# One exponential over three PSUM banks instead of two over two and one, in the attention of an encoder stage

## The reference, cut to what matters

```python
# per layer, x: [16, 256, 128], H = 16 heads, HD = 8
q, k, v = x @ Wq + bq, x @ Wk + bk, x @ Wv + bv     # split into heads
w = softmax(q @ k^T / sqrt(HD), masked)
x = ln(x + (w @ v) @ Wo + bo)
x = ln(x + gelu(x @ W1 + b1) @ W2 + b2)
```

## Time and profile before

| | |
|---|---|
| median of three runs | 5588.78 us (5578.2 to 5590.6) |
| profiled execution, its own time | 5589.84 us |
| its span | 5588.0 us |
| PE busy | 4103.1 us, 73% |
| DVE busy | 2823.0 us, 51% |
| ACT busy | 1910.5 us, 34% |
| POOL busy | 781.6 us, 14% |
| L951 (exponentials), 768 instructions | 580.2 us busy, 529.1 us idle before them |
| L543 (their scores), 3072 matmuls | 403.2 us busy, 80.0 us idle before them |
| L812 (row maxima), 1152 instructions | 747.1 us busy, 356.4 us idle before them |

### The profile page before, as it was taken

How to read it: one execution, slowest core, us unless ns; L and a number is a source line. 1 busy time by engine, 2 the same in 40 slices (tenths; PEclk the granted TensorE clock), 3 DMA queues, 4 the chain that set the end, 5 groups by cost and what they waited for, 6 DMA issues and landing times. The chain is left out here.

```text
span 5588.0 us, 74115 instructions
## 1 busy us (share of the span) xinstructions
PE 4103.1 (73%) x27895; PEld 2767.4 (50%) x27895; DVE 2823.0 (51%) x6809; ACT 1910.5 (34%) x2953; POOL 781.6 (14%) x1090
## 2 busy tenths in 40 slices
PE   5887888888878878879996447885333265887895
PEld 3565665656656656656664114553222233333663
DVE  4655646656556556522213778762455655112662
ACT  2454444544534544433333332212111112221441
POOL 1221222122222212200000000000000022002221
PEclk7998998999989989989997667985565566998995
DMA  4323314224134233000000000000000000002320
GB/s 120 90 52 95 86 49 100 65 72 100 41 94 101 53 85 82 16 35 0 0 0 12 0 0 1 1 1 0 4 0 0 0 3 21 0 0 53 89 70 19
DMA packets 157810, 224.88 MB, mean 40 GB/s; under 512 B 17838, under 2 KB 138030, under 8 KB 140078
## 3 DMA queue, kind: packets, MB, share of 16 engines
q10 hardware_dynamic: 19656, 107.37, 8.6%
q1 hardware_dynamic: 137870, 113.64, 7.4%
HBM read 157.37 MB, written 63.57 MB: 40 GB/s over the span
## 5 line engine op out<-in xcount | busy, mean ns | idle before, releaser
L812 DVE TENSOR_REDUCE enc_mx<-psum 128x2 f32<-128x512 f32 (+1 forms) x1152 | 747.1, 684 | 356.4 <-PE psum L524 353.2
L951 ACT ACTIVATE enc_e<-psum 128x1024 f32<-128x1024 f32 (+1 forms) x768 | 580.2, 808 | 529.1 <-PE psum L543 528.1
L524 PE MATMUL psum<-enc_ks,enc_qs 80*128 80x128 bf16 (+1 forms) x3072 | 475.0, 260 | 112.9 <-DVE enc_mx L812 98.3
L543 PE MATMUL psum<-enc_qs,enc_ks 83*128 83x256 bf16 (+1 forms) x3072 | 403.2, 259 | 80.0 <-DMA enc_qs<-max_pieces 54.3
L524 PEld LDWEIGHTS psum<-enc_ks,enc_qs 80*128 80x128 bf16 x3072 | 227.8, 102 | 244.6 <-DVE enc_mx L812 152.5
L543 PEld LDWEIGHTS psum<-enc_qs,enc_ks 83*128 83x128 bf16 x3072 | 269.4, 103 | 133.8 <-DMA enc_qs<-max_pieces 62.7
L554 PE MATMUL psum<-enc_e,enc_v 128*32 128x256 f32 (+1 forms) x6144 | 334.0, 335 | 0.0
L1608 PEld LDWEIGHTS psum<-par_s,moe_act_h 128*128 128x128 f32 x2304 | 268.6, 192 | 26.8 <-issue 26.8
L1595 PE MATMUL psum<-cur,par_s 128*128 128x512 f32 x576 | 274.0, 622 | 0.0
L68 POOL TENSOR_TENSOR rstd<-vareps,minus_half 128x4 f32<-128x4 f32 x40 | 40.3, 1007 | 1665.8 <-DVE vareps L50 1665.8
L1608 PE MATMUL psum<-par_s,moe_act_h 128*128 128x128 f32 x2304 | 271.5, 275 | 0.0
(11 more groups left out here) (432 smaller groups left out, 8126.4 us busy)
## 6 DMA issues: line engine op xcount, KB each, us to landing
enc_qs<-q_pieces ACTq DMA_DIRECT2D x234, 192.0 KB
enc_ks<-k_pieces ACTq DMA_DIRECT2D x234, 192.0 KB
k_pieces<-enc_pieces SPq DMA_DIRECT2D x240, 128.0 KB, 2.0
q_pieces<-enc_pieces SPq DMA_DIRECT2D x144, 128.0 KB, 2.0
enc_qs<-q_pieces SPq DMA_DIRECT2D x54, 192.0 KB
enc_ks<-k_pieces SPq DMA_DIRECT2D x54, 192.0 KB
rope_qs<-q_pieces ACTq DMA_DIRECT2D x39, 192.0 KB
rope_ks<-k_pieces ACTq DMA_DIRECT2D x39, 192.0 KB
```

The source lines that it names most:

```text
L524: last = T_.matmul(p1[f % 2][:, i * kw:(i + 1) * kw], qs[0:KEYED, slot, h, j * P:(j + 1) * P], ks[0:KEYED, slot, h, 0:kw], start=True, sto ...
L543: last = T_.matmul(p2[ch][:, g], ks[0:SCORED, slot, 4 * T + g, ch * P:(ch + 1) * P], qs[0:SCORED, slot, 4 * T + g, 0:n], start=True, stop= ...
L812: V.tensor_reduce(mx[:, u % 2, j * HEADS + h0:j * HEADS + h0 + n], p1[f % 2].rearrange("p (h k) -> p h k", h=n), AX_X, ALU.max)\
L951: A.activation(e_of(T, ch), p2[ch], ACT.Exp, scale=HD ** -0.5).then_inc(s_e, 1)
```

## The change

`expo` waits once, for both parts of the scores, and makes one activation over the 1536 columns of banks 2, 3 and 4, into the 1536 columns of the half of `enc_e`. It raises `s_e` by two when it is done. `HT * (S + P)` is 4 * 384 = 1536, and column 1024 is where bank 2 begins.

```diff
--- before.py
+++ after.py
@@ -946,9 +946,8 @@
             def expo(layer, u, T):
                 if 4 * u + T >= 2:
                     act.wait_ge(s_pv, at(layer, SEQS * HT, 4 * u + T - 1))
-                for ch in range(JT):
-                    act.wait_ge(s_p2, at(layer, 128, 8 * u + 2 * T + ch + 1))
-                    A.activation(e_of(T, ch), p2[ch], ACT.Exp, scale=HD ** -0.5).then_inc(s_e, 1)
+                act.wait_ge(s_p2, at(layer, 128, 8 * u + 2 * T + 2))
+                A.activation(e[:, T % 2], c.psum[:, 1024:1024 + HT * (S + P)], ACT.Exp, scale=HD ** -0.5).then_inc(s_e, 2)
 
             def move_sums(layer, u, half):
                 act.wait_ge(s_pv, at(layer, SEQS * HT, 4 * u + 2 * half + 2))
```

## The result

The change makes the kernel slower: 5619.53 us as the median of six runs (5610.01 to 5639.43), against 5588.23 (5572.43 to 5590.6, six runs) for the kernel before. The ratio is 1.0065, with a 95% interval of 1.0043 to 1.0086, so 24 to 48 us. The direction is the one forecast, and the size about twice: 15 us were forecast from median to median, and 31 came. The profiled execution took 5610.01 us, the fastest of the six, with a span of 5608.2 us, 20.2 more than before; so the profile shows less than the medians do.

A forecast was written before the change was run, and what follows sets the result against it. Waits, not ScalarE's busy sum, were taken to bound the encoder, even sequences waiting for the fetched maxima. 9.9 + 0.8 + 3.2 = 13.9 us on the profiled 5589.84 gave 5603.7; forecast 5603.5 as a median, range 5586 to 5620.

The forecast's parts named there:

- The instruction: One 1536-column exponential was put at 1453 ns, taken as 1.45 us; ScalarE frees 22 us over 384 blocks, at waiting work.
- The lateness of L940: Block 2, even sequences: the move of the next sequence's maxima comes 0.39 us later (0.38 median), delaying the next start.
- Block 0 costs nothing: Block 0: the one exponential is dispatched at the same 1255.65; 2.4 us of issuing six loads cover its end; no cost.
- From block 2 to the next start: Even sequences 0 to 12: 9.9 us from 26 places where the fetch follows its store by 1.4 us, 0.8 from four.
- the twelve held-up ones: Even sequences whose fetch follows its store by 1.8 to 3.4 us: counted as nothing, upper bound 4.6 us.
- Block 3's scores 0.2 late by their banks: 36 even sequences: block 3's scores wait for banks 2 and 3 and start 0.2 us late, beside the maxima wait.
- block 1's chain over L936 and L796: Block 1, even sequences: L936, L796 and reductions move by 0.38 us, block 3's scores by up to 0.38; covered.
- Sequence 14: No new maxima to make there; L940 and the next sequence come 0.54 us late, six times: 3.2 us.
- Sequence 15: Block 3's scores move 0.64 us, covered by 1.24 us of idleness: nothing, or 3.8 us if that cover is gone.
- odd sequences: Odd sequences 3 to 13: block 3's scores have 2.52 us where 1.6 are needed, maxima 1.2 to spare; no cost.
- a lower clock: Named beside a slower rival: a longer idle stretch can lower TensorE's granted clock, 0.93 in the encoder; no size given.
- every block pays: Rival: odd sequences have no slack either, 36 us, with 5 for sequences 14 and 15: 5631 us; chance 0.16.

The follow-up runs named there:

- split in block 2 alone: The change in blocks 0, 1 and 3, with two exponentials kept in block 2: 5595.6 us against 5587.4 for the kernel before, ratio 1.0015.
- the odd-sequence run: The kernel before with the one exponential in the odd sequences alone: 5591.7 us against 5593.8 for the kernel before, ratio 1.0001.

## Why the prediction was right in sign and short in size

**The instruction** (1453 ns, 22 us freed to no use) was right: 1451 ns, 21 us, and the wait alone without it costs as much.

**The lateness of L940** (0.38 to 0.39) was right in kind and came out as 0.42, since the exponential starts 0.12 us behind the scores instead of 0.09. That this lateness is what passes from block 2 to the next sequence is shown by four runs: merged in block 2 alone, split in block 2 alone, and the maxima moved to either side.

**Block 0 costs nothing: wrong, and the clearest failure.** I argued that the one exponential is dispatched at the same time as the second one before, and that 2.4 us of issuing cover its end. The end is covered; the start of the issuing is not. The load behind it went out 0.10 us later, and everything in block 0 hangs on that issuing, not beside it. By an estimate from the shortest sequences that is 36 x 0.10 = 3.6 us; summed over all 36 it can't be read, since single sequences differ by 1 us either way from profile to profile.

**From block 2 to the next start**, the sum had 9.9 for the 26 clean fetches, 0.8 for four, and nothing for the twelve held-up ones: 10.7 us. Against the one profile of before, the two of the change grew by 12.8 and 12.7, 0.9 and 1.1, and 1.7 and 2.5 us, 15 to 16 in all. But that profile has the lowest sum of the five that keep this part as it was; against their mean the growth is 11 us. The same holds for what the later store saves: the excess of store-to-fetch over 1.40 us, summed over the 42, is 14.9 to 20.2 us in those five (17.4 on average) and 12.4 and 12.2 with the change, so 2.6 us are absorbed by the first count and 5 by the second, where I had let 5.3 go. That the held-up fetches took in most of their lateness was right; whether the term was short at all is not shown.

**Block 3's scores 0.2 late by their banks**: they are 0.34 late, by block 1's chain over L936 and L796, which I had named as the other path. Neither reaches the end, as predicted.

**Sequence 14** 3.2 us: 3.3 and 4.0. **Sequence 15** and the **odd sequences** nothing: no cost of theirs is seen.

**The sum** with these sizes is 9 to 16 for block 2, 3.6 for block 0 and 3.3 to 4.0 for sequence 14: 16 to 24 us, where I had 13.9. The timings gave 31 and 29 us, 25 of them at an equal clock. So the step that failed is, as far as the runs show, the term for block 0 that I put at nothing; 1 to 9 us of the 25 have no term, and why the granted clock was lower in the runs of the change stays open, with the 5 us or so that go with it. I had named a lower clock beside a rival and given it no term of its own. The forecast's range reached to 5620, and the median lies under that by half a microsecond, which is luck. Of the rivals, "every block pays" gave the nearer number for a reason that the odd-sequence run refutes.

## What to carry to other kernels

Before two instructions are merged, look at what waited for the first one's inputs alone, and at what stands behind the second on the same engine: a merge moves the start to the later input, and what stands behind it in the queue moves too. Here the freed time was worth nothing, since ScalarE waited for its inputs in 307 of 384 blocks, and what it freed it spent waiting. And when an engine's queue also issues transfers, look at what stands behind the issuing and what the issuing waits for: here the same profile that gave 0.4 us a sequence to think about showed 3.87 us called issue in front of one copy, and moving the two copies of block 0 ahead of the loads was worth six times what the change cost.

## What the runs showed of the hardware

An activation over a third PSUM bank costs what the second did: 1451 - 1023 = 428 ns for 512 columns, against 1023 - 593 = 430. Where ScalarE is idle, an exponential over 1536 columns starts 0.12 us behind the end of its scores, one over 1024 columns 0.10 us (medians, before and with the change; 0.10 also in the run with one wait and two exponentials, where both wait for the same scores). The load behind the 1536 goes out 0.03 us after its start (1345.29, 1345.32), 0.14 us behind the scores. Behind an exponential that queues up while another runs, the load went out 0.04 us after the scores' end. With one wait and two exponentials it went out at 0.15, so the width of the instruction isn't the cause. I read it as 0.10 us of dispatch that an already running instruction hid, and that waiting with an idle engine exposed; that reading is an argument and not shown.
